# A four-layer convolution kernel on one core: strips stored in the third convolution, row terms between the Hilbert products, and both plane copies on ScalarE

## What is computed

```python
x = x + _L0_conv_ref(_gn(x), w_real, w_imag, b_real, b_imag)   # 3x3 convolution of the 2-D spectrum, and back
x = x + _L1_conv_ref(_gn(x))                                   # gates of 0 or 1 for each row and channel
x = x + _L2_conv_ref(_gn(x), W)                                # 3x3 convolution, 16 to 16 channels
x = x + _L3_conv_ref(_gn(x), weight)                           # 3x3 convolution
```

## Time and profile before

| | us |
|---|---|
| time, median of 3 runs | 4691.74 (4676.85 to 4695.56) |
| time of the profiled execution | 4709.38 |
| its span, first to last instruction | 4707.6 |

### The profile page before, as it was taken

How to read it: one execution, slowest core, us unless ns; L and a number is a source line. 1 busy time by engine, 2 the same in 40 slices (tenths; PEclk the granted TensorE clock), 3 DMA queues, 4 the chain that set the end, 5 groups by cost and what they waited for, 6 DMA issues and landing times.

```text
span 4707.6 us, 229463 instructions
## 1 busy us (share of the span) xinstructions
PE 4279.1 (91%) x85024; PEld 2675.9 (57%) x85024; DVE 3334.5 (71%) x13348; ACT 2540.4 (54%) x8637; POOL 1.0 (0%) x6
## 2 busy tenths in 40 slices
PE   4999988999999998999989999899998999988898
PEld 1455765556655566555655566555665557655476
DVE  2887757876578765887658875688756887578863
ACT  4675526655266543666436654366633666345562
POOL 0000000000000000000000000000000000000000
PEclk8999999999999999999999999999999999999999
DMA  7442015620155202651035510356003650034204
GB/s 190 130 136 76 4 40 171 189 89 4 49 185 182 74 3 62 187 186 54 3 85 183 183 38 3 94 181 187 27 3 108 186 181 14 3 109 139 88 4 146
DMA packets 290246, 468.06 MB, mean 99 GB/s; under 512 B 25536, under 2 KB 92288, under 8 KB 289408
## 3 DMA queue, kind: packets, MB, share of 16 engines
q1 hardware_dynamic: 289536, 457.92, 32.4%
HBM read 323.60 MB, written 134.22 MB: 97 GB/s over the span
## 4 chain that ended last, share of the span: by engine, by line
PE 60%; DVE 12%; DMA 8%; issue 8%; SPq 5%; ACT 3%; DVEq 1%; ACTq 1%
PE ps L1361 34%; PE ps L1255 9%; DMA raw<-x 8%; PE ps L1270 5%; PE ps L1263 3%; PE ps L1279 3%; PE ps L1125 2%; DVE shared L858 2%; SPq L426 2%; SPq L433 2%; DVE xin L853 1%; DVE shared L854 1%; SPq L407 1%; ACT x L584 1%; DVE xin L852 1%
## 5 line engine op out<-in xcount | busy, mean ns | idle before, releaser
L1361 PE MATMUL ps<-x,conv_s 32*32 32x512 f32 x49104 | 1741.9, 606 | 62.4 <-DVE x L1087 30.0
L1361 PEld LDWEIGHTS ps<-x,conv_s 32*32 32x32 f32 x49104 | 1242.5, 104 | 509.5 <-issue 273.7
L1255 PE MATMUL ps<-shared 32*32 32x512 f32 x16384 | 657.4, 604 | 0.0
L1270 PEld LDWEIGHTS ps<-hil,shared 128*128 128x128 f32 x4096 | 504.6, 194 | 194.0 <-issue 193.2
L662 ACT ACTIVATE x<-ps,vec 128x256 f32<-128x256 f32 x512 | 214.6, 470 | 741.4 <-PE ps L1361 741.4
L584 ACT ACTIVATE x<-ps,vec 128x128 f32 (+1 forms) x1024 | 377.6, 385 | 432.2 <-PE ps L1270 431.2
L858 DVE SCALAR_TENSOR_TENSOR shared<-xin,trig 128x128 f32<-128x128 f32 x2048 | 533.8, 301 | 106.7 <-DVE shared L854 98.8
L1279 PE MATMUL ps<-eye,vsb 128*128 128x128 f32 x2048 | 370.7, 305 | 237.1 <-DVE vsb L879 134.1
L1270 PE MATMUL ps<-hil,shared 128*128 128x128 f32 x4096 | 572.5, 284 | 0.0
L1086 DVE SCALAR_TENSOR_TENSOR x<-ps,x 128x256 f32<-128x256 f32 x512 | 214.8, 420 | 427.2 <-ACT x L662 426.2
L1255 PEld LDWEIGHTS ps<-shared 32*32 32x32 f32 x16384 | 310.3, 104 | 278.8 <-issue 213.2
(11 more groups left out here) (204 smaller groups left out, 4711.7 us busy)
## 6 DMA issues: line engine op xcount, KB each, us to landing
out<-x SPq DMA_DIRECT2D x512, 256.0 KB
shared<-x SPq DMA_DIRECT2D x448, 256.0 KB
raw<-x SPq DMA_DIRECT2D x256, 256.0 KB
raw<-x SPq DMA_DIRECT2D x512, 128.0 KB
shared<-t_strip SPq DMA_DIRECT2D x512, 96.0 KB, 4.0
x<-x SPq DMA_DIRECT2D x64, 256.0 KB, 8.8
x<-t_proj SPq DMA_DIRECT2D x1, 2048.0 KB, 11.8
trig<-t_trig SPq DMA_DIRECT2D x1, 512.0 KB, 12.1
```

Of the source, the lines that this page charges most:

```text
L1255: mm = pe.matmul(ps[TM * cg:TM * cg + TM, bank, :], wst[TM * rg:TM * rg + TM, k, v, a, :], of[TM * rg:TM * rg + TM, :], start=(a == AXS), ...
L1270: mm = pe.matmul(quarter(ps[:, BY + 2 * odd + e, :], int(q < 2), q % 2), xt[:, e, q, :], hil[:, q, 0:P], start=False, stop=True, skip_grou ...
L1361: mm = pe.matmul(halves(ps[TM * cg:TM * cg + TM, banks[k], :]), conv_s[TM * rg:TM * rg + TM, kw, second, :], x1b[TM * rg:TM * rg + TM, of, ...
```

## The change

- **Stores.** `DEFERRED` goes from 56 to 8. In the third convolution SyncE stores strips 0 to 35, 36 to 47 and 48 to 55, in small loops, after the loads of pair 0, 1 and 2 of the next image; 8 strips are left for the first four pairs of the next first layer. The third pair of raw strips and tables (`AHEAD` = 3) is thus loaded before the turn of the loop.
- **Planes.** VectorE makes the next image's planes after pairs 17 and 23 instead of 20 and 22. Inside `make_planes` the two raw operations change places, and the waits for them move behind later instructions.
- **Copies.** VectorE's `copy_v` goes; ScalarE copies both mixed planes. On ScalarE, the first transposed strip is copied out before both evictions, the second one after them.
- **TensorE.** `add_u` is called for each strip, right before its own Hilbert products, so the first strip's Hilbert products and transposes stand between the two row products. The mix waits for each strip's eviction apart.

```diff
@@ -27,7 +27,8 @@
 STORES = 16 * STRIPS // STORE_SEMS
-DEFERRED = STRIPS - 2 * UNROLL
+DEFERRED = 2 * UNROLL
+STORED_BY = (36, 48, STRIPS - DEFERRED)
 SIDE = HALF + 2
@@ -39,7 +40,7 @@
 RAW = 2
-U_AT, C_AT, PLANES_AT = (5, 8), (12, 14, 16), (20, 22)
+U_AT, C_AT, PLANES_AT = (5, 8), (12, 14, 16), (17, 23)
 DOT_CREDIT = 2
@@ -416,14 +417,13 @@
-            def store(i, s):
-                k = s % STORE_SEMS
+            def store(i, s, k, turn):
                 sp.wait_ge(evicted, ev(i, 1 + STRIPS + s + 1))
                 sp.sem_inc(s_sp, 1)
-                sp.wait_ge(c_stored[k], (i + 1) * STORES + s // STORE_SEMS * 16)
+                sp.wait_ge(c_stored[k], (i + 1) * STORES + turn * 16)
                 sp.sem_inc(s_sp, 1)
-                sp.dma_start(out[i].rearrange("c (s r) w -> s r c w", r=ROWS)[s], x1[:, s, 0:N]).then_inc(c_stored[k], 16)
+                sp.dma_start(out[i].rearrange("c (s r) w -> s r c w", r=ROWS)[s], x1[:, bass.ds(s, 1), 0:N]).then_inc(c_stored[k], 16)
@@ -438,7 +438,7 @@
-            for pair in range(2):
+            for pair in range(AHEAD):
                 load_pair(0, pair, 2 * pair)
@@ -454,27 +454,27 @@
                     sp.sem_inc(s_sp, 1)
-                for pair in range(2, AHEAD):
-                    load_pair(i, pair, 2 * pair)
-                for pair in range(DEFERRED // 2):
+                for pair in range(PAIRS):
                     feed(pair, 2 * pair % TABLES)
-                    if stores_left:
+                    if stores_left and pair < DEFERRED // 2:
                         for e in range(2):
-                            store(i - 1, STRIPS - DEFERRED + pair * 2 + e)
-                for pair in range(PAIRS - UNROLL, PAIRS):
-                    feed(pair, 2 * pair % TABLES)
+                            s = STRIPS - DEFERRED + pair * 2 + e
+                            store(i - 1, s, s % STORE_SEMS, s // STORE_SEMS)
+                def stores(first, last):
+                    with sp.Fori(first // STORE_SEMS, last // STORE_SEMS) as j:
+                        for k in range(STORE_SEMS):
+                            store(i, j * STORE_SEMS + k, k, j)
                 if more:
-                    for pair in range(2):
+                    stored = 0
+                    for pair, until in enumerate(STORED_BY):
                         load_pair(i + 1, pair, 2 * pair)
-                for n in range(PAIRS):
-                    if more and n >= PAIRS - (STRIPS - DEFERRED):
-                        sp.wait_ge(evicted, ev(i, 1 + STRIPS + 2 * n + 2))
-                        sp.sem_inc(s_sp, 1)
-                        store(i, n - (PAIRS - (STRIPS - DEFERRED)))
-                    elif not more:
-                        for e in range(2):
-                            store(i, 2 * n + e)
+                        stores(stored, until)
+                        stored = until
+                else:
+                    stores(0, STRIPS)
@@ -588,8 +588,9 @@
                     act.wait_ge(mixed, i * PAIRS + pair + 1 + MIXED_CREDIT)
-                    act.wait_ge(turned, t0 + pair * 2 + T_CREDIT)
-                    nc.scalar.activation(vsb[:, 1, :], ps[:, BV + 1, :], ACT.Identity).then_inc(v_copied[1], 1)
+                    for e in range(2):
+                        act.wait_ge(turned, t0 + pair * 2 - 1 + e + T_CREDIT)
+                        nc.scalar.activation(vsb[:, e, :], ps[:, BV + e, :], ACT.Identity).then_inc(v_copied[e], 1)
@@ -608,9 +609,10 @@
                     copy_v(t)
+                    turned_out(t * 2, 0)
                     for e in range(2):
                         evict(t * 2 - 2 + e, e, BY + 2 * (1 - odd) + e, 2 * (1 - odd) + e, uses)
-                        turned_out(t * 2 + e, e)
+                    turned_out(t * 2 + 1, 1)
                     squares(t * 2 - 2, 2 * (1 - odd), uses)
@@ -849,17 +851,20 @@
                     plus, minus = xin[:, k, 0:HALF], xin[:, k, HALF:N]
-                    b.did(V.scalar_tensor_tensor(plus, raw[:, e, 0:HALF], v1(MEAN2), raw[:, e, HALF:N], ALU.subtract, ALU.add))
-                    V.tensor_tensor(minus, raw[:, e, 0:HALF], raw[:, e, HALF:N], ALU.subtract).then_inc(x_taken, 1)
-                    b.then(V.scalar_tensor_tensor(fg(wst[:, k]), fg(mix_s[:, 1]), row_trig[:, 0, bass.ds(s, 1)], fg(mix_s[:, 0]), ALU.mult, ALU.add))
-                    dve.wait_ge(x_taken, i * STRIPS + s + 1 + RAW)
+                    b.did(V.tensor_tensor(minus, raw[:, e, 0:HALF], raw[:, e, HALF:N], ALU.subtract))
+                    V.scalar_tensor_tensor(plus, raw[:, e, 0:HALF], v1(MEAN2), raw[:, e, HALF:N], ALU.subtract, ALU.add).then_inc(x_taken, 1)
+                    b.did(V.scalar_tensor_tensor(fg(wst[:, k]), fg(mix_s[:, 1]), row_trig[:, 0, bass.ds(s, 1)], fg(mix_s[:, 0]), ALU.mult, ALU.add))
+                    b.settle(but=1)
                     for a in range(2):
...
                                                          ALU.mult, ALU.mult, accum_out=gsum[:, 2 * a + q, bass.ds(s, 1)]))
+                        if a == 0:
+                            dve.wait_ge(x_taken, i * STRIPS + s + 1 + RAW)
                         ins = V.tensor_tensor(planes[:, a, k, HALF:N], plus, trig[:, a, 0:HALF], ALU.mult)
...
                             b.did(ins)
+                            b.settle(but=3)
                             b.did(V.scalar_tensor_tensor(fg(wst[:, k]), fg(mix_s[:, 2]), row_trig[:, 1, bass.ds(s, 1)], fg(wst[:, k]), ALU.mult, ALU.add))
@@ -871,12 +876,6 @@
                 t0 = i * STRIPS
-                def copy_v(pair):
-                    dve.wait_ge(mixed, i * PAIRS + pair + 1 + MIXED_CREDIT)
-                    dve.wait_ge(turned, t0 + pair * 2 - 1 + T_CREDIT)
-                    V.tensor_copy(vsb[:, 0, :], ps[:, BV, :]).then_inc(v_copied[0], 1)
@@ -892,7 +891,6 @@
-                    copy_v(pair)
                     make_planes(i, pair + 2, slot)
@@ -904,7 +902,6 @@
                     step(j * 2 + 1, 2)
-                copy_v(PAIRS - 2)
                 dve.wait_ge(b_steps, (t0 + STRIPS) * DVE_B)
@@ -918,8 +915,8 @@
                 ins.then_inc(f_ready, 1)
+                dve.wait_ge(mixed, i * PAIRS + PAIRS - 1 + MIXED_CREDIT)
                 dots(PAIRS - 4)
-                copy_v(PAIRS - 1)
                 for pair in range(PAIRS - 3, PAIRS):
@@ -1239,13 +1236,14 @@
                     due()
-                    pe.wait_ge(y_evicted, t0 + t * 2 - 2) if type(t) is not int or t > 1 else None
-                    due()
                     for e in range(2):
...
                         for e in range(2):
+                            if a == AXS and (type(t) is not int or t > 1):
+                                pe.wait_ge(y_evicted, t0 + t * 2 - 3 + e)
+                                due()
                             k = 2 * odd + e
@@ -1256,12 +1254,11 @@
-                def add_u(t, odd, table, uses):
-                    for e in range(2):
-                        pe.wait_ge(tab_loaded[table + e], (i * (STRIPS // TABLES) + uses + 1) * 16)
-                        pe.matmul(ps[:, BY + 2 * odd + e, :], strip[HP * e:HP * e + HP, table + e, 0:P], u[HP * e:HP * e + HP, :],
-                                  start=False, stop=False, skip_group_check=True)
+                def add_u(e, odd, table, uses):
+                    pe.wait_ge(tab_loaded[table + e], (i * (STRIPS // TABLES) + uses + 1) * 16)
+                    pe.matmul(ps[:, BY + 2 * odd + e, :], strip[HP * e:HP * e + HP, table + e, 0:P], u[HP * e:HP * e + HP, :],
+                              start=False, stop=False, skip_group_check=True)
@@ -1289,8 +1286,8 @@
                     mix(t, odd)
-                    add_u(t - 1, 1 - odd, table, table_uses)
                     for e in range(2):
+                        add_u(e, 1 - odd, table, table_uses)
                         hilbert(t * 2 - 2 + e, e, 1 - odd)
@@ -1310,8 +1307,8 @@
                     step(t, t % 2, (t - 1) // 2, 2 * (t - 1) % TABLES, STRIPS // TABLES - 1)
-                add_u(PAIRS - 1, 1, TABLES - 2, STRIPS // TABLES - 1)
                 for e in range(2):
+                    add_u(e, 1, TABLES - 2, STRIPS // TABLES - 1)
                     hilbert(STRIPS - 2 + e, e, 1)
```

## The result

The changed kernel takes 4728.5 us (median) where the kernel before, in the same comparisons, takes 4697.4: a ratio of **1.0066**, interval 1.0052 to 1.0081. It is slower, as forecast, but by 31 us and not by 107. The profiled execution has a span of 4733.4 us, 25.8 more than the 4707.6 of before.

A forecast was written before the change was run, and what follows sets the result against it. TensorE was taken to set the first layer's pace, its idle time and clock being what can be won. Image 0 +21.7, middle images +17, last +21, third convolutions +47: +107 us on the median, 4799 us, range 4675 to 4870.

The forecast's parts named there:

- Row terms split (1): TensorE, first layer: each row product standing alone costs 1.25 us extra a pair (bounds 0.88 to 1.35), 40 us an image.
- Waits inside the mix (2): TensorE, mix: one more eviction wait between the two strips' products costs 0.05 us (bounds 0 to 0.19), 1.5 us an image.
- TensorE's own work, "8.58 us": First-layer step of image 0: 9.15 us less one wait of 0.57 us leaves 8.58; the new step is 9.88 us.
- the 0.9 us priced for the second eviction: Last image's first layer, without projection: the second eviction starts later and the next mix waits 0.9 us (0.6 now).
- Head of the middle images (6): Start of each middle image, third pair preloaded: 2.4 of 5.67 us idle stay, 2.2 us added to image 0's time (bounds 0 to 5).
- steps 5 and 6: Stores leaving the first layer (gain counted under the copies), and the third preloaded pair with 2.2 us per middle head.
- ScalarE (3): First layer, both copies on ScalarE in new order: waits for ScalarE (0.65 us) and VectorE go; nothing late in images 0 to 6.
- VectorE and the stores (4, 5): First layer: VectorE's lighter load is worth nothing; 48 of 56 stores leave, their gain already counted under the copies.
- Third convolution (7): Third convolutions with a next image: 5 us of "issue" waits plus 1.7 of VectorE waits, 6.7 each, +47 us over seven.
- the free split: Rival: the lone row product fills bubbles or half its time hides, steps of 8.63 us, 4473 us in all; chance 0.12.
- ScalarE as the bound: Rival: ScalarE comes over 1 us late to the copy, steps of 10.2 us, +79 us, 4878 us; chance 0.08.
- The one whose 4713 us lay nearest: Rival: exposed weight loads (-51 us) and third convolution's "issue" waits (-35) both stay away; chance 0.08, one alone 0.12.

The follow-up runs named there:

- e13: The changed kernel with row products together, ScalarE leaving out the larger copy of each first strip's turned planes after the first step: 4480.1 us, ratio 0.9526 to the kernel before.
- e7: The changed kernel with the wait for both evictions ahead of the mix instead of one per strip inside it: 4817.7 us, ratio 1.0255 to the kernel before.
- e3: The changed kernel with the old transfer queue, planes staying at pairs 17 and 23: 4735.5 us, ratio 1.0074 to the kernel before.
- e10: The kernel before with ScalarE's new order and the eviction waits inside the mix, VectorE's copy kept: 4697.3 us, ratio 1.0001.
- e4: The changed kernel with row products together and the old transfer queue: 4546.0 us, ratio 0.9677 to the kernel before.
- e11: The changed kernel with the next image's planes made at 20 and 22 again: 4728.4 us, ratio 1.0062 to the kernel before.
- e6: The kernel before with only the change's transfer queue (stores in the third convolution, three pairs loaded ahead): 4658.8 us, ratio 0.9905.
- e9: The kernel before with only ScalarE's new order (first strip's turning bank emptied before both evictions, second's after): 4737.6 us, ratio 1.0086.
- e1: The changed kernel with both row products of a pair together again, ahead of the first Hilbert product: 4534.8 us, ratio 0.9659 to the kernel before.
- e8: The changed kernel with row products together, projection ahead of the second turn, and ScalarE evicting the first strip before emptying the turning bank: 4519.6 us, ratio 0.9618 to the kernel before.

## Why the prediction was right or wrong

The range held the result; the forecast was 71 us above it. Against the profiled span, +107 was said and +25.8 came: 81 us too much. The direction came out as said, the size did not, and the largest part of the miss is one term, TensorE's own work in a step.

**Row terms split (1): right, one part of it by luck.** The forecast was 1.25 us. The rows give 1.05 for the lone product and 0.57 in place of 0.48 between a turn and what follows, and by the product starts the second Hilbert record follows the first by 0.214 us instead of 0.112: 1.24. The first steps, which hold no wait for an eviction, say the same: 9.58 - 8.34 (e13) = 1.24. The direction held because of this term. Its two open weight loads of 0.10 us were half of 0.66 - 0.47, but that row stands behind a wait: without one the turn takes 0.57, so only 0.10 of the 0.19 was the change of shape and 0.09 came from the wait. The halving gave the right price for a wrong reason.

**Waits inside the mix (2): right in size, wrong in kind.** 0.08 us, within the bounds. That a wait for the eviction stands so close to the start of the mix, and that its new place keeps it small, was not seen (e7).

**TensorE's own work, "8.58 us": the term that failed.** It measured 8.34 us. The prediction took the 0.57 us of idle time in the earlier trace rows off a step of 9.15, as if that were all of the wait. Idle time is counted from the modelled end of the product before, and by the starts the next product can begin sooner. By starts: from the row products at 240.79 it is 1.06, 1.00, 0.47 and 0.89 us (the step of e13) to the second turn, 244.21 where the earlier trace rows has 244.94; and the projection follows 0.66 us later, not 0.57. That is 0.73 + 0.08 = 0.81 us, and 9.15 - 0.81 = 8.34, which e13 showed directly. The new step is 8.34 + 1.25 + 0.08 = 9.67 us (9.66 measured) and not 9.88. Over 30 steps that is 6.3 us; image 0 took 6.0 us less than forecast (317.2 - 311.2), each middle image 6.7 without the head (317.2 - 310.5). The last image held two such waits in a step. Its own work was 8.34 - 1.01 (no projection) = 7.33, not 7.6; its first step takes 8.57, which is 7.33 + 1.25, and the later ones 9.47. Three mixes of image 7, the first step's and the next two:

```profile
4183.94 1.14 PE L1253 MATMUL ps<-xin,shared 32*32 32x512 f32 x32
4192.51 1.70 PE L1253 MATMUL ps<-xin,shared 32*32 32x512 f32 x24
4201.98 1.70 PE L1253 MATMUL ps<-xin,shared 32*32 32x512 f32 x24
```

The starts are 8.57 and 9.47 us apart. In the first mix the products of both strips run on; in the later two only 24 start together and the second strip's come late, and the mix takes 4.23 us for 3.34. So the 0.9 us priced for the second eviction came, though no such wait is listed. There the forecast was 10.3 us too long (313.5 - 303.2). In all 6.0 + 6 x 6.7 + 10.3 = 56 us.

**Head of the middle images (6): wrong, 6 x 2.2 = 13 us.** ScalarE's first copy in image 3, in the change and then in e3, which has the old queue:

```profile
1876.21 1.09 ACT L593 ACTIVATE vsb<-ps 128x512 f32<-128x512 f32 x2 [2.41 <-PE ps L1253]
```

```profile
1870.76 1.09 ACT L593 ACTIVATE vsb<-ps 128x512 f32<-128x512 f32 x2 [4.14 <-issue]
```

In the change ScalarE is there when the mix (begun at 1872.67) ends, 3.5 us later; in e3 it starts 5.2 us after the mix began (1865.58), held by nothing in that row. Over the six middle images it is 3.5 to 3.8 us against 4.9 to 5.5. The packets of the trace point at instructions here too: in e3 each of the six late starts comes 1.5 to 1.6 us after an 8 KB packet of the `q14 instruction` queue has landed, 3.3 to 4.0 us after the mix began; in the change one lands at 1.5 to 1.9 us. The trace doesn't say which engine these packets are for, so this is a reading and not shown. The 2.2 us came from rows in which stores ran, and the same change took the stores away: steps 5 and 6 were never joined.

**ScalarE (3): right.** Both groups of waits went, and it did not become the bound (223 of 311 us busy). The vanished waits of a middle image (30.9 us) and its clock paid for the split, as said: the granted clock there is 0.99 to 1.00 where it was 0.97 to 0.98. e10 shows that for VectorE's group the copy was needed, the order alone left 22.6 us.

**VectorE and the stores (4, 5): right.** The first layer moves 131 GB/s where it moved 173, so the stores are gone from it, and with VectorE's copy gone too this is worth little (e3, e4).

**Third convolution (7): 5.8 us for 6.7, by other parts.** "Issue" waits are 1.9 us on average (0 to 4.4), not 5; VectorE's 35.3 / 7 = 5.0, not 6.0. All listed waits together grew by 2.5 us only; the other 3.3 are in no listed wait but in TensorE's busy time (120.3 to 123.5 us on average), and what lengthened it stays open. By the runs, with the old queue the rest of the change costs 2.1 and 3.0 us (e4, e3), which the prediction gave to the planes' place, and the new queue without that place costs 2.1 and 3.7 (e11, e6). The last image's 6.7 us was no good preview of the others. With 1.9 us that the last image gained, 9 us too much.

By the Trainium skill (Runtime: NRT & Kernel Launch, Instruction fetch mechanics) the fetch of straight-line code is mostly hidden, and the prediction took from it that the stores would be nearly free; the average of 1.9 us is nearer to that than the forecast's 5, and the 4.4 us of image 2 and 7.1 of the last image are not. The Trainium skill (TensorE: Matmul & The Clock Gate, Step-by-step: what each phase is for) would have let weight loads at a change of rows go ahead; the 0.09 and 0.10 us are there in every step, though no run shows that it is the loads that take them.

The terms are 56 + 13 + 9 = 78 of the 81 us; 2.0 more lie in stages that neither kernel changes, and the rest is rounding. Of the rivals, the free split did not come, nor ScalarE as the bound (the free split's -29 us for the last image doesn't follow from its own numbers: 30 steps of 7.6 + 0.05 + 0.9 us and 19.5 are 276 us, which is -17). The one whose 4713 us lay nearest is near by accident: its open loads are there, and only a part of its "issue" waits stayed away. Steps of 9.8 to 9.9 us, a sign that the prediction named for itself, did not come (9.66).

## What to carry to other kernels

Take a wait's price from the starts of the products on both sides, against the same pair of products without the wait, and not from the idle time shown; a step without any idle time can still hold a quarter of a microsecond. Two products that use half of the rows each cost here as much as one of them (1.06 and 1.05 us), so what is put between them costs a whole product. Before pricing an edit, list what stands second in every stage: here the second turn, the eviction and VectorE's copy stood one behind the other, the edits that removed one or two of them gained nothing (e9, e10), and the one that removed all three gained 3.2 to 3.4%, with the old or the new transfer queue (e4, e1).

## What the runs showed of the hardware

- A step with no idle time in the trace held 0.26 us of waiting for another engine (e1 against e13, 8.60 and 8.34 us for the same step).
- By the product starts, Hilbert products and transposes (128 columns) follow each other at 0.11 us; behind a row product, and from the last transpose to a product of another shape, one gap is 0.21 us. Each change of shape in a step costs about 0.1 us, so putting the projection between Hilbert products and turn (e8) gave back a part of what it won.
- Behind the loop's turn ScalarE's first copy started 3.5 to 3.8 us after the first mix in the change's six middle images, with 7 to 86 GB/s in the 6.6 us from the mix on, and 4.9 to 5.5 us in e3's, with 86 to 104 GB/s. The traffic alone doesn't settle it: in e4 two of six start at 3.5 us with 95 GB/s. In images 0 and 7, before whose first layers ScalarE's loop doesn't turn back, it is 3.5 us, at 161 and 13 GB/s.
- Idle time that a view puts down to "issue" can be a wait for instructions: in the third convolutions of the change 20 of 21 such waits of TensorE end 1.3 to 1.7 us after a packet of an instruction queue has landed; over all runs 224 of 237 do, against 10 of 194 waits for VectorE.
- Why these packets come late in some images and not in others, so that the waits vary from 0 to 4.4 us with the same stores, stays open; no run was made for it.
